# Residual pieces and second-norm squares moved from the FFN into the next batch's scores; ctx added by GpSimd, its row sums taken by ScalarE

## The reference

```python
xn = layernorm(x)                       # over the 2048 columns
t, p, g = Wt @ ctx, Wp @ xn, Wg @ ctx   # 512x512 each
att = sum over each of 8 groups of channels and all columns of p * g
y  = blockdiag(Wz) @ (att * t)
x1 = x + groupnorm(y) * gn_w + gn_b + ctx
z  = layernorm(x1)[:, perm] -> 16 heads of 128 columns
out = x1 + unperm( gelu(z_h @ up[h]) @ down[h] )   # 128 -> 512 -> 128 per head
```

## Time and profile before

| | us |
|---|---|
| median of 3 runs | 1608.36 (1607.37 to 1610.45) |
| the profiled execution | 1607.69 |
| its span | 1605.9 |
| TensorE busy | 1518.3 (95%) |
| VectorE busy | 1279.0 (80%) |
| ScalarE busy | 974.7 (61%) |
| GpSimd busy | 874.1 (54%) |

### The profile page before, as it was taken

The page is one execution under the profiler, slowest core; times in us unless marked ns, Lnnn a source line. Parts: engine busy times, 40 slices in busy tenths (PEclk is TensorE's granted clock), DMA queues, the critical chain, the costliest instruction groups (busy, mean ns, idle before and its releaser), DMA issues.

```text
span 1605.9 us, 19290 instructions
## 1 busy us (share of the span) xinstructions
PE 1518.3 (95%) x6592; PEld 1234.1 (77%) x6592; DVE 1279.0 (80%) x1736; ACT 974.7 (61%) x1061; POOL 874.1 (54%) x765
## 2 busy tenths in 40 slices
PE   8998899999989999999999999899998999986997
PEld 6776677877878887788877888688886888765885
DVE  5878979696996879879797888968789697866664
ACT  4334538734776367763677537774487735985785
POOL 1284437157871268613784238832388125976784
PEclk9999999999999999999999999999999999998999
DMA  8788968686776747677386755848568584569685
GB/s 320 288 291 317 331 203 307 247 286 214 239 277 191 251 127 256 248 222 232 118 283 216 249 189 174 283 172 257 163 201 297 156 260 155 190 163 286 207 291 179
DMA packets 126288, 374.77 MB, mean 233 GB/s; under 512 B 24560, under 2 KB 32752, under 8 KB 118000
## 3 DMA queue, kind: packets, MB, share of 16 engines
q1 hardware_dynamic: 91888, 251.88, 47.3%
q0 software_dynamic: 34304, 121.66, 22.4%
HBM read 287.45 MB, written 86.03 MB: 233 GB/s over the span
## 4 chain that ended last, share of the span: by engine, by line
PE 45%; POOL 17%; DVE 17%; DMA 10%; issue 7%; ACT 3%; SPq 0%; POOLq 0%; DVEq 0%; ACTq 0%
PE PP L835 14%; PE PP L849 13%; PE PP L903 7%; PE PP L888 6%; POOL FB L1255 5%; PE PP L862 5%; POOL FB L1252 4%; POOL out L1260 4%; DMA FB<-xg_scratch,perm_sb 3%; DVE R L1017 3%; POOL FB L1240 2%; DVE X L1029 2%; DMA WW<-w_scratch 2%; DVE R L1169 2%; DVE Z L1134 2%
## 5 line engine op out<-in xcount | busy, mean ns | idle before, releaser
L888 PE MATMUL PP<-GG,WW 128*128 128x512 f32 x1536 | 394.2, 393 | 38.8 <-DVE GG L1164 23.4
L835 PE MATMUL PP<-R 128*128 128x512 f32 x1536 | 360.7, 394 | 18.0 <-DVE R L1017 16.2
L888 PEld LDWEIGHTS PP<-GG,WW 128*128 128x128 f32 x1536 | 286.8, 189 | 111.5 <-issue 50.4
L849 PE MATMUL PP<-R,WC 128*128 128x512 f32 x1536 | 352.8, 391 | 7.6 <-ACT Z L934 4.1
L835 PEld LDWEIGHTS PP<-R 128*128 128x128 f32 x1536 | 290.9, 190 | 83.1 <-issue 18.5
L849 PEld LDWEIGHTS PP<-R,WC 128*128 128x128 f32 x1536 | 288.9, 188 | 70.4 <-ACT Z L934 6.8
L903 PE MATMUL PP<-R,WW 128*128 128x512 f32 x1050 | 271.1, 394 | 12.4 <-DMA WW<-w_scratch 6.0
L981 ACT ACTIVATE PP<-PP 128x1024 f32<-128x1024 f32 x256 | 261.6, 1022 | 0.0
L1169 DVE TENSOR_TENSOR R<-PP,R 128x1024 fp32r<-128x1024 f32 x175 | 213.1, 1218 | 60.4 <-ACT PP L981 60.3
L980 ACT ACTIVATE R<-PP 128x1024 fp32r<-128x1024 f32 x175 | 179.7, 1027 | 125.5 <-PE PP L888 125.3
L903 PEld LDWEIGHTS PP<-R,WW 128*128 128x128 f32 x1050 | 195.6, 189 | 58.4 <-issue 17.3
(11 more groups left out here) (91 smaller groups left out, 1639.4 us busy)
## 6 DMA issues: line engine op xcount, KB each, us to landing
WW<-w_scratch SPq DMA_DIRECT2D x152, 512.0 KB, 5.6
X<-in_x SPq DMA_DIRECT2D x32, 1024.0 KB, 5.5
RAW<-in_cx SPq DMA_DIRECT2D x32, 1024.0 KB, 9.2
RAW<-in_xT SPq DMA_DIRECT2D x63, 512.0 KB, 6.3
RAW<-in_cT SPq DMA_DIRECT2D x63, 512.0 KB, 8.6
xg_scratch<-FB POOLq DMA_DIRECT2D x104, 256.0 KB, 6.2
w_scratch<-WW POOLq DMA_DIRECT2D x16, 1024.0 KB, 5.7
RAW<-in_Wg SPq DMA_DIRECT2D x8, 1024.0 KB, 8.3
```

The lines of the kernel that those rows point to most:

```text
L835: t = eng.matmul(s_bank(c1), l[:, part(c1)], r, start=(dt == 0 and j == 0), stop=(dt == ND - 1 and j == 2))
L849: t = eng.matmul(PP[2 + ot // 2][:, ot % 2, :], WC[:, l, ct, part(ot)], u[:, r + ct, :], start=(ct == 0 and j == 0), stop=(ct == NT - 1 an ...
L888: t = eng.matmul(PP[slot["up", f, p]][:, e, :], wt[:, l, part(2 * p + e)], g[:, r, :], start=(j == 0), stop=(j == 2))
```

## The change

For batches 1 to 6 the eight `x1_piece` move from the FFN of batch i into the scores of batch i+1, one every 1.05 units from +0.3, each followed by its square on ScalarE; `load_x` moves with them, and so `bn_x` stands later in the scores. `sum_sq` and what follows it move from +5.4 to +9.6, and `TURN` becomes later and closer. The last batch keeps its places, batch 0 too. `add_c` becomes a plain add on GpSimd that also waits for `bn_x`; a new ScalarE piece `row_c` copies each ctx tile into FB 4 and takes its row sums, so the row sums of ctx come directly and `sum_c` adds those of x to them instead. Weight loads and splits on GpSimd get slightly other due times.

```diff
@@ -24,13 +24,13 @@
 EPS = 1e-5
 NRAW = 3
 NFB = 6
-TURN = [(15.9, 19.0, 22.3, 25.5)] + [(10.2, 15.0, 19.6, 24.2)] * 6
+TURN = [(15.9, 19.0, 22.3, 25.5)] + [(14.3, 17.2, 20.5, 24.0)] * 6
 SBT = 5
+CJ = 4
 UPS = (0, 2, 3)
 S_EARLY = ([(-1 + 0.2 * dt, 0.5 + 0.2 * dt) for dt in range(4)],
            [(2.0, 2.5), (2.25, 2.75), (3.0, 3.25), (3.5, 3.75)])
 S_LOAD = (-13, -10, -7, -2.8, -1, 3.2, 4.8, 6.8)
-X1_UNIT = ((2, 3, 5, 6, 8, 10, 11, 13), (2, 2, 3, 4, 4, 5, 6, 6), (2, 3, 4, 5, 6, 7, 8, 9))
 S_FIRST = ((-5.9, -4.9, -3.9, -2.9), (-9.9, -7.9, -5.9, -3.9))
 S_LATE = {4: 2.55, 5: 2.8, 6: 3.3, 7: 4.4}
 
@@ -176,6 +176,15 @@
     def y_lo(i, q):
         give(n.up("ylo", i, q), ("raw", slot["c", i, q]))
         order.append(("y_lo", i, q))
+
+    def row_c(i, q, ct):
+        if (q, ct) == (0, 0):
+            free["cs", i] = take(("FB", CJ))
+        t = n.up("cs", i, q, ct)
+        give(t, ("raw", slot["c", i, q]))
+        if (q, ct) == (NQ - 1, NT - 1):
+            give(t, ("FB", CJ))
+        order.append(("row_c", i, q, ct))
 
     def add_c(i, q, ct):
         give(n.up("xc", i, q, ct), ("raw", slot["c", i, q]))
@@ -552,7 +561,7 @@
         put(t + 4.1, w_lo, 8 + k)
         put(t + 4.2, keep_w, 8 + k)
     for h in range(4):
-        t = 38 + 4 * h
+        t = 37 + 3.7 * h
         put(t, load_raw, h)
         put(t + 2.6, w_hi, h)
         put(t + 2.7, w_lo, h)
@@ -568,10 +577,10 @@
         y0, v0, f0 = s0 + 16, s0 + 32, s0 + 36
         first = i == 0
         for k, h in enumerate((4, 5, 6, 7) if i == 2 else ()):
-            put(y0 + (2.5, 5.2)[k // 2], load_raw, h)
-            put(y0 + 5.6 + 1.8 * k, w_hi, h)
-            put(y0 + 5.7 + 1.8 * k, w_lo, h)
-            put(y0 + 5.8 + 1.8 * k, keep_w, h)
+            put(y0 + (3.6, 5.6)[k // 2], load_raw, h)
+            put(y0 + 8.0 + 1.8 * k, w_hi, h)
+            put(y0 + 8.1 + 1.8 * k, w_lo, h)
+            put(y0 + 8.2 + 1.8 * k, keep_w, h)
         for j in range(8):
             put(s0 + (S_LOAD[j] if i > 1 else 0.3 if (i, j) == (1, 2) else 2 * j - (5 if i or j else 10)), load_s, i, j)
         for dt in range(ND):
@@ -582,24 +591,25 @@
                 put(s0 + (dt + 0.25 * c1 if i < 2 or dt > 3 else S_EARLY[c1 // 2][dt][c1 % 2]), s_mm, i, dt, c1)
         for q in range(NQ):
             for ct in range(NT):
-                t = s0 + 2.2 + 3.3 * ct + 0.8 * q if i == 2 else s0 + (4 * q + ct) * 0.85 + 0.9
+                t = s0 + 6 + 2.1 * ct + 0.4 * q + (1.9 if ct == 3 else 0)
                 t = 10.4 + 1.4 * ct + 0.22 * q if first else s0 + 9.3 + 1.6 * ct + 0.4 * q if i == 1 else t
                 put(t, bn_x, i, ct, q)
         if first:
             for ct in range(NT):
                 put(5.4 + 1.7 * ct, load_x, i, ct)
-        put(y0 + 2, aggr_x, i)
-        put(y0 + 2.1, root_x, i)
+        put(y0 + 2.2, aggr_x, i)
+        put(y0 + 2.3, root_x, i)
         late = 1.0 if i == 1 else 0
         for q, t in enumerate((s0 + 9, s0 + 11, s0 + 13, y0 + 1.5 + late)):
             put(t, load_c, i, q)
-        put(y0 + (9 if i == 2 else 2.5 + late), load_wg, i)
+        put(y0 + (9 if i == 2 else 4.2 + late), load_wg, i)
         for q, t in enumerate((y0 - 3, y0 + 0.4, y0 + 4.3, y0 + 8.3)):
             put(t, y_hi, i, q)
             put(t + 0.2, y_lo, i, q)
         for q, t in enumerate((y0 - 1, y0 + 1.2, y0 + 2.6, y0 + 4.6)):
             for ct in range(NT):
-                put(t + 0.25 * ct + late, add_c, i, q, ct)
+                put(t + 0.25 * ct + late, row_c, i, q, ct)
+                put(max(t, y0 + 2 * q) + 0.45 * ct + late, add_c, i, q, ct)
         put(y0 + 5.8 + late, sum_c, i)
         put(y0 + 5.9 + late, store_sum, i)
         put(y0 + 7.6 + late, spread_sum, i)
@@ -633,13 +643,13 @@
         last = i == B - 1
         for k in range(8):
             ct, hf = k // 2, k % 2
-            t = f0 + 5 + 0.8 * k if first else f0 + 3.25 + 2 * X1_UNIT[1 if i == 1 else 2 if last else 0][k] + 0.01 * k
+            t = f0 + 5 + 0.8 * k if first else f0 + 3.25 + 2 * (k + 2) if last else base[i + 1] + 0.3 + 1.05 * k
             put(t, x1_piece, i, ct, hf)
-            put(t + (0.9 if first else 1.2) if first or last else base[i + 1] + 0.9 + 0.55 * k, square_x1, i, ct, hf)
+            put(t + (1.2 if last else 0.9), square_x1, i, ct, hf)
             if hf and not last:
-                put(base[2] - 1.5 + 3.3 * ct if i == 1 else t + 0.1, load_x, i + 1, ct)
+                put(t + 0.1, load_x, i + 1, ct)
         put(f0 + (4.1 if first else 5.26), mean_x1, i)
-        e = f0 + 12 if first else f0 + 22.8 if last else base[i + 1] + 5.4
+        e = f0 + 12 if first else f0 + 22.8 if last else base[i + 1] + 9.6
         put(e, sum_sq, i)
         put(e + 0.1, root_x1, i)
         put(e + 0.9, shift_x1, i)
@@ -926,6 +936,16 @@
                 for t in free["yhi", i, q]:
                     act.wait_ge(*t)
                 eng.copy(R[slot["y", i, q]][:, 0:4, :], RAW[slot["c", i, q]][:]).then_inc(S["yhi"], 1)
+            elif stage == "row_c":
+                i, q, ct = a
+                act.wait_ge(*at["c", i, q])
+                if (q, ct) == (0, 0):
+                    for t in free["cs", i]:
+                        act.wait_ge(*t)
+                else:
+                    act.wait_ge(*at["cs", i, q - (ct == 0), (ct - 1) % NT])
+                eng.activation(FB[:, CJ, :], RAW[slot["c", i, q]][:, ct, :], ACT.Identity, scale=1.0,
+                               accum_out=sxc[:, ct, q:q + 1]).then_inc(S["cs"], 1)
             elif stage == "y_ev":
                 i, q, pr = a
                 act.wait_ge(*at["ymm", i, q, 2 * pr + 1])
@@ -1022,22 +1042,15 @@
                 u = R[slot["y", i, q]]
                 eng.tensor_tensor(u[:, 4:8, :], RAW[slot["c", i, q]][:], f32(u[:, 0:4, :]),
                                   ALU.subtract).then_inc(S["ylo"], 1)
-            elif stage == "add_c":
-                i, q, ct = a
-                dve.wait_ge(*at["c", i, q])
-                dve.wait_ge(*at["x", i, ct])
-                eng.tensor_tensor_reduce(out=X[:, ct, cols(q)], in0=X[:, ct, cols(q)],
-                                         in1=RAW[slot["c", i, q]][:, ct, :], scale=1.0, scalar=0.0, op0=ALU.add,
-                                         op1=ALU.add, accum_out=sxc[:, ct, q:q + 1]).then_inc(S["xc"], 1)
             elif stage == "sum_c":
                 i = a[0]
-                dve.wait_ge(*at["xc", i, NQ - 1, NT - 1])
+                dve.wait_ge(*at["cs", i, NQ - 1, NT - 1])
                 dve.wait_ge(*at["mv1", i, NT - 1])
                 for t in free["scol", i]:
                     dve.wait_ge(*t)
-                eng.tensor_reduce(scol[:, 0, :], sxc[:], AXIS.X, ALU.add).then_inc(S["sst"], 1)
+                eng.tensor_reduce(scol[:, 1, :], sxc[:], AXIS.X, ALU.add).then_inc(S["sst"], 1)
                 dve.wait_ge(*at["sst", i, 0])
-                eng.scalar_tensor_tensor(out=scol[:, 1, :], in0=mv1[:, :, 0], scalar=-float(D), in1=scol[:, 0, :],
+                eng.scalar_tensor_tensor(out=scol[:, 0, :], in0=mv1[:, :, 0], scalar=float(D), in1=scol[:, 1, :],
                                          op0=ALU.mult, op1=ALU.add).then_inc(S["sst"], 1)
             elif stage == "s_fix":
                 i, c1 = a
@@ -1244,6 +1257,13 @@
                 pool.wait_ge(*at["tr", i, q, NT - 1])
                 for r in range(4):
                     eng.dma_start(xg_rows(i, q, r), tb_part(i, q, r)).then_inc(S[f"xg{q}"], 16)
+            elif stage == "add_c":
+                i, q, ct = a
+                pool.wait_ge(*at["c", i, q])
+                pool.wait_ge(*at["x", i, ct])
+                pool.wait_ge(*at["bn1", i, ct, NQ - 1])
+                eng.tensor_tensor(X[:, ct, cols(q)], X[:, ct, cols(q)], RAW[slot["c", i, q]][:, ct, :],
+                                  ALU.add).then_inc(S["xc"], 1)
             elif stage == "resid":
                 f, b = a
                 pool.wait_ge(*at["ghi", f])
@@ -1339,7 +1359,7 @@
                     S[f"w{w % 2}{j}"], 16)
             elif stage == "store_sum":
                 i = a[0]
-                sp.wait_ge(*at["sst", i, 1])
+                sp.wait_ge(*at["sst", i, 0])
                 eng.dma_start(vs_d[i].rearrange("(p t) -> p t", p=P), scol[:, 1, :]).then_inc(S["vs"], 16)
             elif stage == "spread_sum":
                 i = a[0]
```

## The result

The changed kernel takes 1680.93 us (median of 4 runs, 1678.7 to 1682.81) against 1609.4 us for the kernel before, measured beside it: ratio 1.0427, 95% interval 1.040 to 1.0453, or 71.5 us. The forecast was 1652, so the direction and the mechanism named first were right, and the size was 29 us short. Spans: 1679.5 us after, 1605.9 before.

What follows compares the result with a forecast made beforehand. TensorE sets the pace, except in each FFN's second half, where VectorE does. From 1607.69 us, -26.5 (FFN and first y products) and +70 (six y stages) gave 1651, forecast as 1652; range 1606 to 1686.

Steps and rivals of the forecast that it cites:

- The FFN: In FFN 2 to 6, TensorE's waits on VectorE go when x1_piece leaves: 4.9 us won each, 24.5 us in all.
- The scores: In the scores, sum_sq comes at 894.7, not 882.42, and shift_x1 at 897.1; the stage itself loses 0 to 2 us.
- The transposes: In y, turns waiting for stores delay y_lo 2 and 3: 9.1 us, with other costs 11.6 per stage, 70 in six.
- L: Time from a transposed piece's first store start to its last landing in y, taken as 8.2 us.
- the 0.6 before v: At the end of each y stage, s_fix and s_evl queued behind y_lo 3 cost 0.6 us more before v.
- The adds and row sums: In y, GpSimd's 22 us of adds fit but in order; a late ctx load's row sums hide behind y_lo 2.
- an end of +3: Pessimistic end of the -2 us for y of batches 0 and 1: GpSimd splits weights there and 16 operations delay g_root.
- The lock that my sum left out: VectorE and GpSimd exclude each other on shared SBUF ports; each y_lo could lose one add, 1.3 us, uncounted.
- Rival 1: Stores in y land in time, L under 5.2 us leaving y_lo 3 not late: faster, 1587 us; chance 0.13.
- Rival 2: Unloaded stores in y, L = 7.0 and no clock drop: +11 us, 1619; chance 0.17.
- Rival 3: L of 9 or more, late fourth ctx load, scores 2 us late, GpSimd overloaded in batch 2: 1686 us; chance 0.12.
- Rival 4: FFN not freed: waits on L1164 move to GpSimd or the gathers, costing up to 20 us of the gain; no chance given.

Runs made afterwards that it cites:

- Experiments 8 to 12: Kernel before, adds on VectorE, with two, four, six or all eight x1_piece of batches 2 to 6 packed early into the next scores: ratios 0.9854 to 0.9919.
- experiment 2: Changed kernel with only two of each piece's four transpose stores made in batches 3 to 6: 1663.75 us, ratio 1.0306.
- the kernel with six moved: Kernel before with six x1_piece of batches 2 to 6 packed at the start of the next scores, adds on VectorE: 1589.28 us, ratio 0.9854.
- the adds alone: Changed kernel with residual pieces, bn_x, sum_sq and TURN back at their old places; adds on GpSimd, row sums on ScalarE kept: 1677.97 us, ratio 1.0398.
- experiment 6: The run with the adds alone, but from batch 3 GpSimd's adds of pieces 2 and 3 stand behind its stores of piece 2: 1667.09 us, ratio 1.0325.

## Why the prediction was right in kind and short in size

**The FFN.** Right, and too small: -31.7 for -24.5 us. FFN 2 to 6 won 6.3 us each instead of 4.9; TensorE is busy all through (39.84 of 40.1 us in the second half). I had kept 1.4 us of waits that also went. `x1_piece` in its new place takes 1.28 us, as forecast.

**The scores.** Right on every step: `sum_sq` 0.65 us, `shift_x1` 0.14 and the end of the turns 0.1 us from the forecast, the stage 46.4 us long. But I read the lateness as what eight pieces cost. Experiments 8 to 12 say otherwise: it is the places written. In the change `sum_sq` is due at 9.6, eight `bn_x` and 13 of the 16 `s_lo` stand ahead of it (six and eight before), and the pieces are spread at 1.05 units. Those places (pieces, `bn_x`, `sum_sq`, `TURN`) were changed together; which of them carries most wasn't tried.

**The transposes.** The mechanism was right: waits on `y_lo` 2 and `y_lo` 3, about two per stage of 3.7 to 8 us, VectorE waiting 125.0 us for stores, the clock at half after it. The size: +14.9 us per stage (89.4 in six) for 11.6. In batch 5 L was 8.8 (952.49 to 961.31), 7.1 and 10.1 us, 1.4 more than three times 8.2; `y_lo` 2 took 3.39 us for 2.2 beside a GpSimd add, and the stores of piece 2 started 0.5 late behind seven adds. `y_lo` 3 thus ended at 992.9 and not at 951.0 + 38.7 = 989.7: 3.2 us. The clock then cost 2.7 us (13.66 for 10.9) and not 1.7; the 0.6 before v did not come (y ends and v begins as before). This is the first mis-sized term, 19 us.

**The adds and row sums.** Here a step failed: "It fits, but in order." An add costs 1.40 us and `row_c` 0.82, about what I took, but cover by busy time was not cover by order. In batches 0 and 1 I forecast -2 us and +10.7 came, in batch 2 another 2.9 us (its v took 5.1 longer, its scores 2.0 less): 15.6 us. I had seen that the row sums would hold ScalarE for a late ctx load and put it behind the later `y_lo`; in batches 0 and 1 there is no late `y_lo` ahead of it, so it was the wait. `g_root`, which I had as an end of +3, was the other: 6.60 us on VectorE and 5.33 on TensorE in the scores of batch 1. The lock that my sum left out is in the first two terms: it stretched a `y_lo` to 3.39 us in the changed kernel and to 8.92 in experiment 2.

**The rivals.** Rival 1, the stores land in time, holds in the kernels of experiments 8 to 12 and not in this one: not because L was smaller (10.7 us for piece 0 in the kernel with six moved, from 891.68 to 902.41), but because the turns end 12 us earlier against y. By the fit that the Trainium skill gives ("DMA: Bandwidth & Descriptors") L would be near 4.7, an estimate; in batches 2 to 7 it was 6.9 to 11.6 for pieces 0 to 2, and the trace doesn't agree. Rival 2, unloaded stores and no clock drop, had 1619 and fell. Rival 3, more than the transposes, was the nearest to what came, 1686 for 1681; its late ctx load and its GpSimd in batch 2 were there, its 2 us in the scores were not. Rival 4, the FFN not freed, fell.

**What stays open.** What makes the stores of piece 2 land 3.2 us slower with the adds alone, and how much of their 4.7 us of late start is the lock, which stretches the adds ahead of them, and how much the order: experiment 6 took out part of the order and won 1.3 us of them, where one stage can differ by 3 from run to run. How much of batches 0 and 1 is `row_c` and how much the adds wasn't tried either.

## What to carry to other kernels

In an in-order schedule, price the place of a moved piece, not only its work: ask which chain starts behind it (here the sum of squares, the normalising, the transposes, the stores, the next transposes, the splits) and put the head of that chain as early as before; the same eight pieces cost 5.7% in one order and won 0.8% in another (where those of batch 1 stayed). Freed time on an engine is of use only ahead of what the bound engine waits for, and a moved operation on a slack engine must be checked against each DMA issue, each slot release and each eviction queued behind it. When a wait goes and the time stays, look at the other queue that the same late event feeds.
